# Transposes of the mixer that go to two PSUM banks in turn

## The reference

```python
proj = einsum(x, in_proj_w)               # gate (8192), hBC (8192 + 2048), dt (128)
hBC = silu(causal_conv4(hBC) + conv_b)    # 4 taps along the sequence, each channel by itself
hs, Bm, Cm = split(hBC)                   # hs: 128 heads of 64
Y = Y_diag + Y_off + hs * D               # chunks of 128 tokens: (C B^T * decay) x, and C prev_state
g = Y * silu(gate)
out = groupwise_rmsnorm(g, 8 groups) * norm_w
return einsum(out, out_proj_w)            # 8192 -> 512
```

## Time and profile before

| | before |
|---|---|
| median of 3 runs | 2715.9 us |
| lowest, highest | 2715.47, 2716.67 us |
| the profiled execution, its own time | 2718.86 us |
| its span, first to last instruction | 2717.1 us |
| mean granted TensorE clock | 0.981 |
| first and last transposes of convolution blocks | at 1112.8 and 2539.6 us of the span |

### The profile page before, as it was taken

The page is one execution under the profiler, slowest core; times in us unless marked ns, Lnnn a source line. Parts: engine busy times, 40 slices in busy tenths (PEclk is TensorE's granted clock), DMA queues, the critical chain, the costliest instruction groups (busy, mean ns, idle before and its releaser), DMA issues.

```text
span 2717.1 us, 58923 instructions
## 1 busy us (share of the span) xinstructions
PE 2567.2 (94%) x19678; PEld 2041.7 (75%) x19678; DVE 1867.5 (69%) x2720; ACT 1364.3 (50%) x2492; POOL 1431.7 (53%) x1404
## 2 busy tenths in 40 slices
PE   4999999999999669899999999999999999999989
PEld 3778787787787448677777777777777777777777
DVE  5675766766757668767777677577676677785874
ACT  3434434334334245655664665665566646656621
POOL 1654655556546110456656656476575566574720
PEclk8999999999999869999999999999999999999999
DMA  2010110110110014211111111101111111111011
GB/s 89 24 50 27 34 44 23 44 40 19 51 36 12 17 66 138 88 33 44 40 33 58 37 38 49 38 29 52 43 38 50 33 58 34 41 49 38 18 47 47
DMA packets 72632, 118.79 MB, mean 44 GB/s; under 512 B 10310, under 2 KB 22214, under 8 KB 72373
## 3 DMA queue, kind: packets, MB, share of 16 engines
q1 hardware_dynamic: 72388, 115.61, 13.0%
HBM read 102.92 MB, written 12.65 MB: 43 GB/s over the span
## 4 chain that ended last, share of the span: by engine, by line
PE 48%; issue 4%; DVE 4%; POOL 2%; ACT 2%; DVEq 0%; POOLq 0%; ACTq 0%
PE proj L218 10%; PE proj L220 10%; PE proj L219 10%; PE core_y L1403 5%; PE core_o L1409 2%; PE turned L252 2%; DVE mx_acc L1214 2%; PE turned L1430 2%; PE decay L1462 1%; PE mx_decay L1462 1%; POOL mx_acc L1663 1%; PE mx_decay L220 1%; PE mx_decay L218 1%; PE mx_decay L219 1%; POOL mx_th L1660 1%
## 5 line engine op out<-in xcount | busy, mean ns | idle before, releaser
L201 DVE TENSOR_TENSOR slab_lo<-slab_raw,slab_hi 128x512 fp32r<-128x512 f32 (+2 forms) x272 | 256.9, 957 | 147.4 <-ACT slab_hi L192 121.6
L218 PE MATMUL proj<-slab_hi,XTL 128*128 128x512 f32 x816 | 355.0, 435 | 0.0
L218 PE MATMUL proj<-XTH,slab_lo 128*128 128x512 f32 x736 | 300.0, 408 | 37.5 <-PEq L81 14.4
L220 PE MATMUL proj<-slab_hi,XTH 128*128 128x512 f32 x816 | 320.7, 393 | 0.0
L219 PE MATMUL proj<-slab_lo,XTH 128*128 128x512 f32 x816 | 318.5, 390 | 0.0
L220 PE MATMUL proj<-XTH,slab_hi 128*128 128x512 f32 x736 | 292.3, 397 | 0.0
L219 PE MATMUL proj<-XTL,slab_hi 128*128 128x512 f32 x736 | 292.0, 397 | 0.0
L1660 POOL TENSOR_TENSOR mx_th<-mx_th,mx_acc 128x512 f32<-128x512 f32 x48 | 62.1, 1294 | 369.0 <-ACT mx_th L1560 368.9
L1677 POOL TENSOR_TENSOR mx_gate<-mx_gate,mx_hd 128x512 f32<-128x512 f32 x128 | 171.1, 1336 | 156.4 <-DVE mx_hd L1591 145.4
L218 PE MATMUL proj<-slab_hi,mx_otl 128*128 128x512 f32 x576 | 241.9, 420 | 0.0
L220 PE MATMUL proj<-slab_hi,mx_oth 128*128 128x512 f32 x576 | 227.7, 395 | 0.0
(11 more groups left out here) (351 smaller groups left out, 6719.5 us busy)
## 6 DMA issues: line engine op xcount, KB each, us to landing
slab_raw<-in_w_gate SPq DMA_DIRECT2D x64, 256.0 KB, 3.0
slab_raw<-in_w_out SPq DMA_DIRECT2D x64, 256.0 KB, 3.0
slab_raw<-in_w_x SPq DMA_DIRECT2D x60, 256.0 KB, 3.6
slab_raw<-in_w_q SPq DMA_DIRECT2D x32, 256.0 KB, 3.0
slab_raw<-in_w_g SPq DMA_DIRECT2D x32, 256.0 KB, 3.0
slab_raw<-in_w_o SPq DMA_DIRECT2D x32, 256.0 KB, 2.9
bc_scratch<-bc_acc SPq DMA_DIRECT2D x32, 256.0 KB, 2.0
slab_raw<-in_w_bc SPq DMA_DIRECT2D x20, 256.0 KB, 4.5
```

The lines of the kernel that those rows point to most:

```text
L201: op = nc.vector.tensor_tensor(K.SL[par][:, c, 0:width], K.RAW[c][:, 0:width], hi, ALU.subtract)
L218: nc.tensor.matmul(to[:, 0:bh.shape[-1]], al, bh, start=(c == 0), stop=False)
L220: mm = nc.tensor.matmul(to[:, 0:bh.shape[-1]], ah, bh, start=False, stop=(c == KC - 1))
```

## The change

`PT` and the so far idle `PX` become a pair `TB`. The transposes of convolution block u go to `TB[u % 2]`, those of tile t to `TB[t % 2]`, and each waits for the reader two groups back in place of the last one. Blocks 0 and 1 follow on the wait for all low parts of the half before (block 1 has no wait of its own for a bank), tiles 0 and 1 on all eight copies to HS. In the last half tile 7 stays in `PT`, where tile 6 was turned, with the wait for tile 6's low part as before. The readers (L260, L265, L1522) take the bank as an argument. No instruction that computes is added or removed.

```diff
-def turn_tile(nc, K, pe, m, src, free, count):
+def turn_tile(nc, K, pe, m, src, free, count, bank=None):
+    bank = K.PT if bank is None else bank
     pe.wait_ge(K.y_ready, HEAD + m + 1)
     pe.wait_ge(free, HEAD + count)
     for r in range(KC):
-        tr = nc.tensor.transpose(K.PT[:, r * P:(r + 1) * P], ...
+        tr = nc.tensor.transpose(bank[:, r * P:(r + 1) * P], ...
...
+        TB = [K.PT, PX]
+
+        def turned_in(last, s, t):
+            return K.PT if last and s == 1 and t == 7 else TB[t % 2]
...
                     if r in TURN:
                         t = TURN.index(r)
-                        turn_tile(nc, K, pe, m + t, GT[t % GRING], K.ot_lo if t else S["mx_hs"], m + t if t else NT * q + 8)
+                        free, count = (K.ot_lo, m + t - 1) if t >= 2 else (S["mx_hs"], NT * q + 8)
+                        if last and s == 1 and t == 7:
+                            count = m + 7
+                        turn_tile(nc, K, pe, m + t, GT[t % GRING], free, count, turned_in(last, s, t))
                     if 4 <= sl < 12:
                         u = sl - 4
                         pe.wait_ge(S["mx_cm"], HEAD + NT * q + u + 1)
                         if u == 0:
                             pe.wait_ge(K.ot_lo, HEAD + m)
-                        else:
-                            pe.wait_ge(S["mx_hs"], HEAD + NT * q + u)
+                        elif u >= 2:
+                            pe.wait_ge(S["mx_hs"], HEAD + NT * q + u - 1)
                         for k in range(4):
-                            tr = nc.tensor.transpose(K.PT[:, k * P:(k + 1) * P], ...
+                            tr = nc.tensor.transpose(TB[u % 2][:, k * P:(k + 1) * P], ...
                         tr.then_inc(S["mx_hsT"], 1)
```

More of the change, by code:

```diff
@@ L251, in turn_tile, with tile_hi, tile_lo @@
     for r in range(KC):
-        tr = nc.tensor.transpose(K.PT[:, r * P:(r + 1) * P], src[:, r * P:(r + 1) * P], K.ident[:, :])
+        tr = nc.tensor.transpose(bank[:, r * P:(r + 1) * P], src[:, r * P:(r + 1) * P], K.ident[:, :])
     tr.then_inc(K.turned, 1)
-def tile_hi(nc, K, act, m, t, out_unit):
+def tile_hi(nc, K, act, m, t, out_unit, bank=None):
     act.wait_ge(K.turned, HEAD + m + 1)
     act.wait_ge(K.unit_done, HEAD + out_unit)
-    nc.scalar.activation(K.OTH[t % 2][:, :, :].rearrange("p r n -> p (r n)"), K.PT[:, :], ACT.Copy).then_inc(K.ot_hi, 1)
-def tile_lo(nc, K, dve, m, t):
+    nc.scalar.activation(K.OTH[t % 2][:, :, :].rearrange("p r n -> p (r n)"), (K.PT if bank is None else bank)[:, :],
+                         ACT.Copy).then_inc(K.ot_hi, 1)
+def tile_lo(nc, K, dve, m, t, bank=None):
     dve.wait_ge(K.ot_hi, HEAD + m + 1)
-    return nc.vector.tensor_tensor(K.OTL[t % 2][:, :, :].rearrange("p r n -> p (r n)"), K.PT[:, :],
+    return nc.vector.tensor_tensor(K.OTL[t % 2][:, :, :].rearrange("p r n -> p (r n)"), (K.PT if bank is None else bank)[:, :],
                                    K.OTH[t % 2][:, :, :].rearrange("p r n -> p (r n)").bitcast(F32),
@@ L1426, in half @@
                             pe.wait_ge(K.ot_lo, HEAD + m)
-                        else:
-                            pe.wait_ge(S["mx_hs"], HEAD + NT * q + u)
+                        elif u >= 2:
+                            pe.wait_ge(S["mx_hs"], HEAD + NT * q + u - 1)
                         for k in range(4):
-                            tr = nc.tensor.transpose(K.PT[:, k * P:(k + 1) * P], acc[u % 4][:, k * P:(k + 1) * P], K.ident[:, :])
+                            tr = nc.tensor.transpose(TB[u % 2][:, k * P:(k + 1) * P], acc[u % 4][:, k * P:(k + 1) * P], K.ident[:, :])
                         tr.then_inc(S["mx_hsT"], 1)
@@ L1510, in half @@
                         prev = u0 + out_slot[t - 2] + 1 if t >= 2 else u0 - SLOTS + out_slot[t + 6] + 1
-                        tile_hi(nc, K, act, m + t, t, prev)
+                        tile_hi(nc, K, act, m + t, t, prev, turned_in(last, s, t))
                         if s == 0 and t == 0:
@@ L1522, in half @@
                         nc.scalar.activation(HS[:, 4 * (u // 4):4 * (u // 4) + 4, (u % 4) * P:(u % 4 + 1) * P],
-                                             K.PT[:, :].rearrange("p (t n) -> p t n", t=4), ACT.Copy).then_inc(S["mx_hs"], 1)
+                                             TB[u % 2][:, :].rearrange("p (t n) -> p t n", t=4), ACT.Copy).then_inc(S["mx_hs"], 1)
                     if s == 0 and sl == 8:
@@ L1579, in half @@
                     if r in TURN:
-                        tile_lo(nc, K, dve, m + TURN.index(r), TURN.index(r))
+                        t = TURN.index(r)
+                        tile_lo(nc, K, dve, m + t, t, turned_in(last, s, t))
                     if s == 0 and sl in (4, 6):
```

## The result

| | before | after |
|---|---|---|
| median | 2715.9 us (7 runs, 2714.3 to 2721.0) | 2706.75 us (7 runs, 2703.4 to 2709.3) |
| ratio | | 0.9962, 95% interval 0.9952 to 0.9972 |
| profiled execution, span | 2718.86, 2717.1 us | 2708.85, 2707.1 us |
| granted TensorE clock | 0.981 | 0.979 |

The changed kernel is faster by 0.38%, 7.6 to 13.0 us by the interval of the ratio. The forecast was 13.0 us; the median moved 9.2 us and the span 10.0 us. Single runs of one program differ by 6 us and more, so a total says less than the stretches of a trace. The granted clock goes with these differences: of the 24 runs of the kernel before that were taken beside the first experiments, the slowest (2724.1 us) had a mean of 0.977 and the three fastest (2712.4 to 2713.3 us) had 0.981 to 0.983.

What follows compares the result with a forecast made beforehand. TensorE, busy 94% of the span, was taken as the bound, with time won only where it stands still. 8.16 + 2.64 + 2.66 - 0.49 = 12.97 us took the median from 2715.9 to 2702.9 us; range 2697 to 2710.

Steps and rivals of the forecast that it cites:

- Block 1: Transposes of convolution block 1 in odd halves: their only wait for a bank goes, gain 8.16 us.
- Block 6: Transposes of convolution block 6 in odd halves: they need block 4's copy, two slots old, gain 2.64 us.
- Tile 7 and o6: Seven odd halves: tile 7's wait moves to unit o6, which needs tile 6's low part; only 2.66 us won.
- Block 4: Odd halves: TensorE arrives earlier and waits for GpSimd's silu, 0.07 us lost 7 times, 0.49 us.
- The first chunk product: Odd halves, waits for VectorE's mask product: cost taken as 0, bounds 0 and 0.84 us.
- the full 0.84 us: Odd halves: how much earlier VectorE must reach the mask product so that the first chunk product costs nothing.
- Rival (a): All bank waits vanish, tile 7's too, with 1.15 in place of 0.38 us there: 18.4 us, 2697.5 us; 6%.
- Rival (b): ScalarE and VectorE don't follow and the first chunk product of odd halves waits: 7.1 us gain, 2708.8 us; 10%.
- Rival (d): Slower: in slots 5 to 10 of odd halves VectorE meets more GpSimd operations, 1.1 us each: 2722.2 us; 5%.
- Even halves: Block 0's wait for silu, behind VectorE's 4.82 us idle, should move with TensorE: no gain, no loss.
- Its sign: In the trace after, block 0 of even halves still waits 1.5 us.
- Rival (c): No change: odd halves' gain is waited off at block 0 of the next even half: 2715.2 us; 9%.

Runs made afterwards that it cites:

- tiles only: Against the kernel before, only the turned tiles take two banks in turn, the blocks stay in `PT`; median 2716.85 us, ratio 0.9998 (0.9987 to 1.0008).
- written out: The kernel before, with the mixer's hardware loop over seven groups written out on all five queues; median 2693.35 us, ratio 0.9917 (0.9901 to 0.9934).

## Why the prediction was right, and where it was off

**Odd halves.** All terms, as lost time on TensorE summed over the eight odd halves. Block 1: 8.1 us predicted 8.16. Block 6: 2.65, predicted 2.64. Tile 7 and o6: tile 7 lost 9.0 us less, o6 5.8 us more, so 3.2 us won where 2.66 was predicted; that the wait moves to o6 was the decisive step and it held, in the change and in tiles only. Block 4 was to lose 0.49 us for GpSimd's silu: it lost nothing, but block 2 lost 0.9 us, 0.23 us in four of seven halves. The first chunk product was taken at 0: it lost 0.10 to 0.13 us in four halves, 0.4 us in sum. The last chunk product of odd halves won 0.5 us, which the sum did not have. Together 13.1 us, predicted 12.97. That the sums agree within 0.2 us is partly luck: tile 7, block 4 and the last chunk product came out 1.5 us better than predicted in sum, block 2 and the first chunk product 1.3 us worse.

**Block 2** is late by the same meeting of VectorE and GpSimd as in the earlier trace rows, with the other outcome. In the changed kernel, half 7, VectorE and GpSimd:

```profile
1769.67 0.68 DVE L201 TENSOR_TENSOR slab_lo<-slab_raw,slab_hi 128x512 fp32r<-128x512 f32 x1
```

```profile
1769.65 1.86 POOL L1673 TENSOR_TENSOR mx_acc<-mx_th,mx_acc 128x512 f32<-128x512 f32 x1
```

Both begin within 0.02 us. The split takes 0.68 us, and the silu that block 2 awaits 1.86 in place of 1.29 us: this time GpSimd was held. In the kernel before it was VectorE:

```profile
1775.34 1.80 DVE L201 TENSOR_TENSOR slab_lo<-slab_raw,slab_hi 128x512 fp32r<-128x512 f32 x1
```

```profile
1775.29 1.29 POOL L1663 TENSOR_TENSOR mx_acc<-mx_th,mx_acc 128x512 f32<-128x512 f32 x1
```

In the seven odd halves that the changed kernel has in the loop the two go together without exception: where the split took 0.68 us (four halves) block 2 was late, where it took 1.81 or 1.82 us (three) it was not. The rule of the Trainium skill (SBUF — State Buffer, Who interferes with whom) is that the shared ports go to one of the two engines at a time, and that the order of issue decides who is blocked. The rows agree with the first part. They do not show the second: GpSimd's row starts first in both, by 0.02 and 0.05 us, and it was held in one of them. The prediction had priced only the case in which VectorE loses. VectorE also did not gain the full 0.84 us ahead of the chunk product: by the end of the mask product it was 0.58 us earlier, and 0.53 + 0.58 = 1.11 us is 0.1 less than the lead that TensorE had. Its silu in that stretch took 1.34 us and had taken 1.06.

**Rival (a)**, all bank waits vanish: out, by o6. The Trainium skill (Perfetto Trace Analysis, Optimization Strategy) names too few buffers as a possible reason for a gap that repeats. The traces agree for blocks 1 and 6, where the second bank won all 10.8 us, and not for tile 7, where 5.8 of the 9.0 us came back at o6. **Rival (b)**: a trace of it, 0.4 us of the 5.9 (7 x 0.84) that it priced. **Rival (d)**: new meetings there were, at block 2, but they cost 0.9 us and not 3 us a half.

**Even halves**, "no gain, no loss", held in the profiled pair: heads 97.5 and 97.2 us, and between block 0 and o7 the even halves differ by 0.3 us in sum. Its sign, that block 0 waits for silu as long as before, did not hold: 2.6 us of that wait went ahead of x0. I had seen the 4.82 us before VectorE's first operation of a group and left open what they were. They belong to the jump back: VectorE has such an idle time, 2.96 to 4.82 us, at each of the six jumps and at none of the same places written out. The head there takes 15.1 to 16.9 us in the kernel before and 13.7 without a jump. Its single places differ by over 1 us from one execution to the next, and in the second profile of the changed kernel the six took 1.4 us more than before. Rival (c) had that place, though its price, all of the gain, did not occur with this change.

**Where it was off** is the total: the forecast of 2702.9 us is 3.9 us under the measured median, outside the forecast's own range of about 2700 to 2706 and inside the range of the prediction. The sum of 13.0 us is right for the mixer of the profiled pair (1500.5 and 1487.5 us from the first x0 to the last o7). The step that carried it over to the median assumed that nothing else differs between two executions. Outside the mixer the two profiles of the changed kernel differ from the one before by 3 us more and 4.5 us less, with the lower clock for more or less time. So one pair of profiles cannot place a median to within 3 us. The medians came out 9.2 us (7.6 to 13.0 by the ratio) and 8.9 us (5.7 to 12.5) faster; why both lie under 13 is not settled beyond the 1.4 us of the heads.

## What to carry to other kernels

A second bank removes a wait only as far as the next instruction in the queue does not need the same reader: look at who stands behind the waiting instruction before counting its whole idle time. Where the releaser is a queue that did something less urgent first, its order may be the cheaper and larger cure, as for tile 7 here. And measure a gain of a few microseconds by stretch as well as by total: behind it may lie a place, here the jump of a hardware loop with a large body, that is long and varies. Where a stretch grows, look at the pace of its matmuls and the granted clock before calling it idle time.

## What the runs showed of the hardware that was not expected

The jump back of a loop over a body of some 1800 matmuls costs 1.4 to 3.4 us each time over straight code (heads of 15.1 to 17.1 against 13.7 us, where the clock stayed at its full level). The idle time stands ahead of x0, ahead of block 0 or in parts at both. Written out, with the same computing instructions, the program is 23 us faster: 15 us from the heads, 8 us from odd halves, where block 1 loses 0.39 in place of 1.11 us and tile 7 0.9 in place of 1.37 us in five of seven.

A stall of 1.93 to 2.50 us on a TensorE that was otherwise busy was followed in six cases by 3.4 us at the lower level of the clock, at 0.43 us from matmul to matmul, which cost 1.5 to 1.7 us on top of the stall. Behind three others of that size (2.15, 2.24, 2.28 us) the clock stayed up.

Two operations of VectorE and GpSimd that start within 0.05 us of each other may go either way, and which one is held (0.68 or 1.8 us, 1.29 or 1.86 us) differs between halves of one execution. In the changed kernel GpSimd's row starts first in all seven, by 0.01 to 0.02 us where GpSimd was held and by 0.02 to 0.04 us where VectorE was. In the last half VectorE's row starts 0.10 us ahead, and GpSimd was held (1.73 us).
